# RWKV time mixing with a SwiGLU block on one core: the order of the V and R projections, one round's scaling, and the engine of the third exponent

## The reference, cut to what matters

```python
# x: 1 x 4096 x 256, fp32; L0_attn, then L0_ffn (hidden 768, int8-valued weights in int32)
def _wkv(w, u, k, v):                      # scan over 4096 steps, per channel
    def step(carry, kv):
        aa, bb, pp = carry
        kt, vt = kv
        ww = u + kt
        q = jnp.maximum(pp, ww)
        e1 = jnp.exp(pp - q); e2 = jnp.exp(ww - q)
        y = (e1 * aa + e2 * vt) / (e1 * bb + e2)
        ww2 = pp + w
        q2 = jnp.maximum(ww2, kt)
        e1 = jnp.exp(ww2 - q2); e2 = jnp.exp(kt - q2)
        return ((e1 * aa + e2 * vt, e1 * bb + e2, q2), y)
xx = shift x by one step
k, v, r = (x * mix_i + xx * (1 - mix_i)) @ W_i.T     # i = k, v, r
rwkv = sigmoid(r) * _wkv(-exp(time_decay), time_first, k, v)
x = layernorm(x + rwkv @ Wo.T)
x = layernorm(x + (silu(x @ wg.T) * (x @ wu.T)) @ wd.T)
```

## Time and profile before

| | |
|---|---|
| median of three runs | 310.6 us (309.38 to 312.05) |
| the profiled execution | 310.04 us |
| its span, first to last instruction | 308.2 us |
| busy | PE 274.2 (89%), DVE 273.1 (89%), ACT 217.1 (70%), POOL 147.9 (48%) |
| rounds 3, 4, 5 and 6 | 33 us each, from 104 to 236 us |
| mean granted TensorE clock | 0.962 |

### The profile page before, as it was taken

The page is one execution under the profiler, slowest core; times in us unless marked ns, Lnnn a source line. Parts: engine busy times, 40 slices in busy tenths (PEclk is TensorE's granted clock), DMA queues, the critical chain, the costliest instruction groups (busy, mean ns, idle before and its releaser), DMA issues.

```text
span 308.2 us, 4400 instructions
## 1 busy us (share of the span) xinstructions
PE 274.2 (89%) x1250; PEld 198.8 (64%) x1250; DVE 273.1 (89%) x484; ACT 217.1 (70%) x386; POOL 147.9 (48%) x123
## 2 busy tenths in 40 slices
PE   7588569942999999999999999999999999999991
PEld 5334456712689467955786477746793679868790
DVE  5999798726999999999999999999989999989673
ACT  3488577328976698659775888569865976399384
POOL 3556344647384727481739155743846172006030
PEclk9989599995899999999999999999999999999998
DMA  7902200031110400122022201030102002101003
GB/s 254 323 2 68 69 2 1 0 136 23 48 35 2 102 35 14 55 68 70 0 70 55 82 0 68 0 102 0 68 0 68 1 0 70 34 2 68 0 4 106
DMA packets 13523, 16.24 MB, mean 53 GB/s; under 512 B 704, under 2 KB 11200, under 8 KB 13504
## 3 DMA queue, kind: packets, MB, share of 16 engines
q1 hardware_dynamic: 12816, 15.48, 15.8%
q10 hardware_dynamic: 688, 0.53, 0.5%
HBM read 11.81 MB, written 4.19 MB: 52 GB/s over the span
## 4 chain that ended last, share of the span: by engine, by line
DVE 35%; PE 23%; ACT 20%; issue 15%; DMA 2%; DVEq 1%; POOL 1%; ACTq 0%; SPq 0%; POOLq 0%
DVE state L658 6%; PE bank_a L1026 5%; DVE stats L703 5%; PE bank_a L1003 4%; PE bank_b L1003 3%; DVE wts L629 3%; ACT x L433 3%; DVE res L716 3%; ACT act L484 3%; DVE pmax L612 2%; ACT wts L410 2%; PE bank_c L961 2%; DVE res L765 2%; PE bank_b L980 2%; DVE kv L652 2%
## 5 line engine op out<-in xcount | busy, mean ns | idle before, releaser
L347 POOL TENSOR_TENSOR hlo<-hid,hhi 128x512 fp32r<-128x512 f32 (+1 forms) x36 | 54.3, 1511 | 46.3 <-ACT hhi L492 46.2
L332 POOL TENSOR_TENSOR mix<-mix,xt 128x512 f32<-128x512 f32 x48 | 56.7, 1212 | 12.9 <-ACT mix L418 12.9
L418 ACT ACTIVATE mix<-dx,par 128x512 f32<-128x512 f32 x48 | 31.2, 711 | 25.3 <-POOL dx L326 25.3
L1026 PE MATMUL bank_a<-wd_r,hhi 128*128 128x256 f32 x192 | 46.5, 285 | 0.6 <-ACT act L484 0.2
L1026 PE MATMUL bank_a<-wd_r,hlo 128*128 128x256 f32 x192 | 45.2, 278 | 0.0
L339 POOL TENSOR_TENSOR den<-wts,state 128x512 f32<-128x512 f32 x14 | 16.7, 1194 | 55.7 <-DVE state L646 55.7
L492 ACT ACTIVATE hhi<-hid 128x512 fp32r<-128x512 f32 (+1 forms) x54 | 31.1, 578 | 12.4 <-DVE hid L749 12.2
L1026 PEld LDWEIGHTS bank_a<-wd_r,hhi 128*128 128x128 f32 x192 | 36.0, 188 | 3.6 <-issue 2.5
L1026 PEld LDWEIGHTS bank_a<-wd_r,hlo 128*128 128x128 f32 x192 | 36.0, 188 | 0.3 <-issue 0.2
L410 ACT ACTIVATE wts<-wts 128x512 f32<-128x512 f32 (+1 forms) x54 | 28.0, 578 | 8.5 <-DVE wts L629 8.5
L1003 PE MATMUL bank_a<-x1hi,wg_r 128*128 128x512 f32 (+1 forms) x96 | 32.0, 414 | 1.4 <-ACT act L484 0.9
(11 more groups left out here) (103 smaller groups left out, 548.1 us busy)
## 6 DMA issues: line engine op xcount, KB each, us to landing
xt<-xT SPq DMA_DIRECT2D x7, 513.0 KB, 3.7
xrow<-x SPq DMA_DIRECT2D x7, 512.0 KB, 3.8
out<-y SPq DMA_DIRECT2D x6, 512.0 KB, 2.8
wg_i<-wg SPq DMA_DIRECT2D x1, 768.0 KB, 8.6
wu_i<-wu SPq DMA_DIRECT2D x1, 768.0 KB, 10.1
wd_i<-wd SPq DMA_DIRECT2D x1, 768.0 KB, 11.8
out<-y SPq DMA_DIRECT2D x3, 256.0 KB, 2.1
xt<-xT SPq DMA_DIRECT2D x2, 257.0 KB, 2.9
```

The source lines that it names most:

```text
L332: nc.gpsimd.tensor_tensor(mix[:, s, i, h, 0:n], mix[:, s, i, h, 0:n], xt[:, h, 0:n], ALU.add).then_inc(mixed, 1)
L347: nc.gpsimd.tensor_tensor(hlo[:, m, 0:n], hid[:, m % NH, 0:n], hhi[:, m, 0:n].bitcast(f32), ALU.subtract).then_inc(hlo_ready, 1)
L418: nc.scalar.activation(mix[:, s, i, h, 0:n], dx[:, h, 0:n], ACT.Copy, scale=par[:, MIX + i, h:h + 1]).then_inc(dx_scaled, 1)
L1026: mm = nc.tensor.matmul(ffn[:, q, :], hp.bitcast(f32) if full else hp, w[:, m, :], start=(m == 0 and q % 2 == 0 and part is hhi), stop=(m ...
```

## The change

Four edits.

- PE: in rounds 2 to 7, half 0 of V of the next chunk stands between `down` and `attention_out`, half 1 behind K. Half 0 of R takes its place ahead of the transposes, half 1 stays behind them (in round 7 the whole of R was ahead of them and is).
- The OUT argument of every chunk moves from DVE (`exp_args`) to POOL (`out_arg`), with a semaphore of its own. In rounds 2 to 7 it stands at the end of POOL's round, in round 1 between `dx` and the mixes of chunk 3, for chunks 0 and 1 in the opening part.
- Chunk 2's K is scaled and mixed one round earlier, behind V; only R remains in round 1. On ACT round 1's `first_norm` stands ahead of the scaling of chunk 3, which comes last in the round.
- POOL's rounds 3 to 6 are written out instead of looped.

```diff
+            def out_arg(c, h):
+                pool.wait_ge(gap_ready, c * CH + (h + 1))
+                n = steps(c)
+                nc.gpsimd.tensor_scalar(wts[:, OUT, h, 0:n], gap[:, h, 0:n], par[:, FIRST, h:h + 1], CAP, ALU.add,
+                                        ALU.min).then_inc(out_arg_ready, 1)
...
-                if isinstance(j, int) and j == 1:
-                    mix_chunk(2, 0, (K, R))
+                if j == 1:
+                    mix_chunk(2, 0, [R])
                 if ahead:
                     pool.wait_ge(rwkv_ready, j + 1)
                     diffs(j + 2)
-                    mix_chunk(j + 2, s)
+                    if j > 1:
+                        mix_chunk(j + 2, s)
+                if not last(j):
+                    out_arg(j + 1, 0)
+                    out_arg(j + 1, 1)
+                if j == 1:
+                    mix_chunk(3, s)
...
+            pool.wait_ge(par_in, 16)
+            out_arg(0, 0)
             diffs(1)
+            out_arg(0, 1)
             mix_chunk(1, 1)
             pool.wait_ge(wd_in, 16)
             nc.gpsimd.tensor_copy(wd_r[:, :, :], wd_i[:, :, :]).then_inc(wd_ready, 1)
+            out_arg(1, 0)
+            out_arg(1, 1)
             diffs(2)
-            mix_chunk(2, 0, [V])
+            mix_chunk(2, 0, [V, K])
...
                 if isinstance(j, int) and j == 1:
-                    scale_chunk(2, 0, (K, R))
+                    scale_chunk(2, 0, [R])
+                    first_norm(j, nxt)
+                    scale_chunk(3, s)
+                    return
...
                     nc.scalar.activation(wu_r[:, :, :], wu_i[:, :, :], ACT.Copy).then_inc(wu_ready, 1)
+                    scale_chunk(2, 0, [K])
...
-                for i in which:
-                    s = par[:, FIRST, h:h + 1] if i == OUT else decay[:, h:h + 1]
-                    nc.vector.tensor_scalar(wts[:, i, h, 0:n], gap[:, h, 0:n], s, CAP if i == OUT else 0.0, ALU.add,
+                for i in (IN_NEW, IN_OLD):
+                    nc.vector.tensor_scalar(wts[:, i, h, 0:n], gap[:, h, 0:n], decay[:, h:h + 1], 0.0, ALU.add,
                                             ALU.max if i == IN_OLD else ALU.min).then_inc(args_ready, 1)
...
+                v_beside = nxt and not (isinstance(j, int) and j < 2)
+                if v_beside:
+                    project(j + 1, s, V, [0])
                 if not last(j):
                     attention_out(j)
                 if nxt and not first(j):
                     project(j + 1, s, K)
-                    if not (isinstance(j, int) and j == 1):
-                        project(j + 1, s, V)
+                if v_beside:
+                    project(j + 1, s, V, [1])
                 if first(j) or last(j + 1):
                     project(j + 1, s, R)
-                if isinstance(j, int) and j == 1:
+                elif nxt:
                     project(j + 1, s, R, [0])
...
                 if nxt and not first(j) and not last(j + 1):
-                    project(j + 1, s, R, [1] if isinstance(j, int) and j == 1 else range(CH))
+                    project(j + 1, s, R, [1])
```

More of the change, by code:

```diff
@@ L182, in rwkv_swiglu_kernel @@
         args_ready = sem("args_ready")
+        out_arg_ready = sem("out_arg_ready")
         wts_ready = sem("wts_ready")
@@ L396, in _ @@
             round_(2, 0, True, True)
-            with pool.Fori(3, NC - 2, 2) as j:
-                round_(j, 1, True, True)
-                round_(j + 1, 0, True, True)
+            for j in range(3, NC - 2):
+                round_(j, j % 2, True, True)
             round_(NC - 2, 1, True, False)
@@ L407, in weight @@
             def weight(c, i, h):
-                sc.wait_ge(args_ready, c * (NW * CH) + (h * NW + i + 1))
+                if i == OUT:
+                    sc.wait_ge(out_arg_ready, c * CH + (h + 1))
+                else:
+                    sc.wait_ge(args_ready, c * (2 * CH) + (h * 2 + i + 1))
                 n = steps(c)
@@ L620, in gaps, with exp_args @@
                                         ALU.subtract).then_inc(gap_ready, 1)
-            def exp_args(c, h, which=range(NW)):
+            def exp_args(c, h):
                 dve.wait_ge(gap_ready, c * CH + (h + 1))
                 n = steps(c)
-                for i in which:
-                    s = par[:, FIRST, h:h + 1] if i == OUT else decay[:, h:h + 1]
-                    nc.vector.tensor_scalar(wts[:, i, h, 0:n], gap[:, h, 0:n], s, CAP if i == OUT else 0.0, ALU.add,
+                for i in (IN_NEW, IN_OLD):
+                    nc.vector.tensor_scalar(wts[:, i, h, 0:n], gap[:, h, 0:n], decay[:, h:h + 1], 0.0, ALU.add,
                                             ALU.max if i == IN_OLD else ALU.min).then_inc(args_ready, 1)
@@ L820, in round_ @@
                     range_flag()
-                    exp_args(1, 1, [IN_NEW, IN_OLD])
+                    exp_args(1, 1)
                     wide_flag()
                     norm_rows(0, x1, res1, mv1, rstd1, rstd1_ready, x1_ready, halved(0))
-                    exp_args(1, 1, [OUT])
                     x1_low(0, 0)
@@ L843, in round_ @@
                 shift_rows2(j - 1)
-                exp_args(j + 1, 1, (IN_NEW, IN_OLD))
+                exp_args(j + 1, 1)
                 x1_low(j, 0)
                 x1_low(j, 1)
-                exp_args(j + 1, 1, [OUT])
             def range_flag():
```

## The result

The changed kernel takes 312.78 us (median of nine, 311.32 to 313.91) against 310.26 us for the kernel before on the same chip. The ratio is 1.0087, 95% interval 1.0064 to 1.0110: slower by 0.9%. The forecast was 306.1 with a range of 301.0 to 311.5: the time lies above the range, and the direction was wrong. The profiled execution took 312.31 us with a span of 310.4, against 310.04 and 308.2.

A forecast was written before the change was run, and what follows sets the result against it. DVE was taken to set the pace (busy 31.95 of 33.00 us in round 5). Opening -3.5, hole -4.7, OUT +1.0, V +1.3 +1.0 +0.4 sum to -4.5: 305.5 us profiled, 306.1 median, range 301.0 to 311.5.

The forecast's parts named there:

- Half of V: Ahead of the output product: DVE waits 1.2 us; costs 0.33 in rounds 3 to 6, 1.0 in round 2, 0.4 in round 7.
- OUT in the rounds: POOL's OUT arguments in rounds 2 to 6: 0.62 lost, 0.40 saved on DVE, +0.2 us a round, +1.0 together.
- d: Time of one OUT argument as a tensor_scalar on POOL, taken as 0.8 us, between 0.49 and 1.1.
- the second DVE argument ends at 205.28 + 2d + 0.46: Round 5: DVE's second argument waits for both POOL OUT arguments, instead of ending at 206.58; `x1hi` comes 2d - 0.98 later.
- POOL's OUT arguments are slow: Rival, rounds 2 to 6: d over 1.24 us turns the change to a loss; 314.2 us with d = 1.6; chance 0.15.
- The opening: Rounds 0 and 1 before the hole: OUT arguments off DVE gain 3.5 us, between 1.5 and 4.8.
- `x1hi` at about 33.8: Opening, chunk 1: ACT finishes scaling V, the cast of `wu` and scaling K by about 33.8, against 38.36 for `x1hi` before.
- the 2.2 us for chunk 0: Opening: chunk 0's recurrence can start some 3 us earlier, of which DVE keeps about 2.2 since K of chunk 1 waits.
- The hole: End of round 1: the norm no longer waits for chunk 3's scalings; 4.7 us left as gain, between 3.5 and 5.7.
- the first step: Hole of round 1: `dx` of chunk 3 stays at 66.2, but `shift` ends at 63.4 instead of 72.78, 9.4 us earlier.
- the payback: What comes off the hole's 9.4 us: later `dx`, ACT's scalings, mixes beside round 2's scans and POOL's queue, leaving 4.7.
- The ring: Round 2: product 5 waits in the ring of three for POOL's `hlo` 2, done at 85.8; 1.0 us, between 0 and 2.2.

## Why the prediction was wrong

- **Half of V: the mechanism was right, its term mis-sized.** The wait of 1.2 us, expected at the second residual sum, was 1.39 at the first and 0.17 at the second. Of the two outcomes worked out (0.1 if the copy catches the gap between mixes, 0.66 if it misses) I took half. It misses in every round: measured 0.7 in rounds 3 to 6 for 0.33, 1.9 in round 2 (0.8 on top of the other edits) for 1.0, 0.7 in round 7 for 0.4. The order alone costs 5.3 us where the sum had 2.7. Where POOL's loop is written out, round 6 loses 1.3, since the gain of that edit is then partly lost.
- **OUT in the rounds: d was wrong, and the step from d to the time too; that its term came out small was luck.** d was taken as 0.8 us and measures 2.0 to 2.3. By the step "the second DVE argument ends at 205.28 + 2d + 0.46" a d of 2.2 would cost 3 us a round. It costs 0 against before (32.96 for 32.95) and 0.1 against the same kernel with OUT on DVE: the two arguments beside it take 0.94 us for 0.87, and the 0.40 us that DVE saves behind `x1lo` are lost again in the copy of the state, 0.58 for 0.17. The pattern of `dx`, 2.36 us for 0.87, was carried to POOL's tensor_scalar, which has one tensor operand, and for DVE's arguments it doesn't hold there; for the copy it does. The Trainium skill (SBUF: State Buffer, Who interferes with whom), on which the rival leaned, says of the ports that GpSimd and DVE's two-port modes share that the one who starts first keeps them for its whole instruction. This trace disagrees for POOL's tensor_scalar, since both DVE arguments of 206.89 to 207.83 lie inside one of POOL's (206.47 to 208.77). That DVE's arguments run in such a mode no run shows, but beside `dx` they did wait. The rival "POOL's OUT arguments are slow" thus had the duration and the sign of the result right and its mechanism wrong.
- **The opening: the step "`x1hi` at about 33.8" failed, and so did the 2.2 us for chunk 0.** The first priced ACT's queue and left out POOL's: two OUT arguments of 4.08 us stand ahead of `dx` of chunk 2, on which V's scalings wait, and K's stand behind them. `x1hi` starts at 36.78. As for chunk 0, `rwkv` of round 0 starts 0.2 us earlier (0.55 with OUT alone): DVE waits 1.03 us for the exponential of POOL's OUT of half 1 and then has two scans that take 2.80 us for 1.38. OUT alone still brings 3.3 us at `rwkv` of round 1, about the forecast's 3.5, but without K and with most of it in chunk 1, so that number was luck. K early takes back 2.4: 1.3 by the later start of the copy, 0.7 by its wait beside K's mixes, the rest behind it. Measured -1.0 for -3.5.
- **The hole: the first step was right, the payback too small.** The shift ends at 62.25 (63.4 less the opening's gain), `xt` stands behind `xrow` as said, and products 4 and 5 wait for POOL as said. But the first product's wait is 3.72 us for 2.0, because POOL's OUT arguments end at 71.7 and not 69.1, and ACT's last exponential, the scalings and the table load come later with them. With OUT on DVE the wait is 1.97, about the forecast's. The ring costs 1.81 + 0.57 for 1.0, behind mixes of 8.23 us for 6.9 and `den` of 3.25 for 2.3. Measured -1.8 for -4.7; with OUT on DVE it is -2.9, so 1.1 of the missing 2.9 belong to OUT and 1.8 to the queue on POOL. PE's clock at 0.50 in 78 to 84 wasn't in the sum, and it isn't what DVE waits for: in the run with only the order of round 1 the clock is back at 1.00 from 82 on, and the waits in the ring are the same, 1.83 and 0.54.
- **The loop written out had no term.** It is the fourth edit of the change, and the prediction passed over it. It gives 1.3 us in round 6 without the V order and 0.7 with it. Since it is a gain, it hid part of the loss.
- **Right:** the 0.36 us ahead of the transposes, the queue behind `xrow`, the clock of the warming matmuls, the band of 33.0 to 33.9 us for rounds 3 to 5 (round 6 took 32.99). Of the signs named, three failed: POOL's tensor_scalar at 0.7 to 0.9 us, the second argument of half 0 on DVE at over 1 us, and a wait of over 1 us at the second residual sum, since it stands at the first.

In us of the profiled execution: opening -1.0, hole -1.8, round 2's end +1.8, rounds 3 to 5 +2.1, round 6 0.0, round 7 +0.9, tail +0.2, against a forecast of -3.5, -4.7, +1.2, +1.6, +0.5, +0.4 and 0. Of the 6.7 us between them, 5.4 are the opening and the hole.

## What to carry to other kernels

When a stall goes, follow the transfer behind it: unless it is issued earlier, the work that hangs on it lands in the next stage, in queues that were free before. Here a give-back of 9.5 us became none once the transfer was brought forward and the mixes ahead of it moved, with a smaller gain at the stall itself. Filling PE ahead of the product that the pacing engine waits for costs that engine's wait in every round, however full PE gets; and two edits that each gain can lose it again where their instructions queue on the same engine, so try them apart. Where a loop is written out, look for a last pass whose size shrinks.
